# A recurrent retention block with a mixture of experts: TensorE's program written out over the layers instead of looped

## The reference, cut to what matters

```python
xn = _layernorm(x, axis=-1)                  # x: 8 samples x 512 tokens x 128
s = attn(xn)                                 # L = 4 layers, one after the other
g = _silu(ffn(xn))                           # top-1 mixture of 8 experts, 128 -> 512 -> 128
return x + s * g

def block(h, p):                             # one layer of attn, scanned over the 4 layers
    r = _retention(h, wk)                    # k, q, v; tril(q k^T), row sums, times v
    m = r @ w1 + b1
    a, gate = jnp.split(m, 2, axis=-1)
    m = a * jax.nn.silu(gate) @ w2 + b2
    m = _groupnorm1(m, gg, gb)
    y = m + h
    f = jax.nn.gelu(y @ wf1 + bf1_, approximate=False) @ wf2 + bf2_
    return (_layernorm(f + y, lg, lb), None)
```

## Time and profile before

| | us |
|---|---|
| median of 3 runs | 535.2 (534.99 to 535.72) |
| span of the profiled execution, first to last instruction | 533.2 |
| the profiled execution's own time | not recorded apart from its span |
| TensorE matmuls, busy | 478.8 (90% of the span) |
| VectorE, busy | 387.6 (73%) |
| ScalarE, busy | 264.7 (50%) |
| GpSimd, busy | 262.9 (49%) |
| mean granted TensorE clock | 0.958 of full speed |

### The profile page before, as it was taken

One profiled execution on the slowest core, in us unless ns is written; L12 is line 12 of the kernel. 1 busy time (PEld: TensorE's weight loads), 2 busy tenths in 40 slices (PEclk: granted clock), 3 DMA queues, 4 the chain that ended last, 5 costly groups with the idle time before them and its releaser, 6 DMA issues.

```text
span 533.2 us, 11094 instructions
## 1 busy us (share of the span) xinstructions
PE 478.8 (90%) x3179; PEld 399.0 (75%) x3180; DVE 387.6 (73%) x1343; ACT 264.7 (50%) x565; POOL 262.9 (49%) x349
## 2 busy tenths in 40 slices
PE   6998889999999999996999999996999999999610
PEld 4886666667888898884898888884888888986410
DVE  4668888888777777774677777775577777786896
ACT  3823244444555555661556565661466555655630
POOL 4472388886454444441444443442345344434664
PEclk9999999999999999997999999998999999999665
DMA  9999411115111010111011010111011011113213
GB/s 255 235 114 260 131 35 36 36 36 92 51 57 43 34 57 31 56 59 35 22 45 56 31 61 32 55 61 40 6 56 61 32 56 37 55 37 104 65 39 119
DMA packets 48844, 36.30 MB, mean 68 GB/s; under 512 B 13960, under 2 KB 39888, under 8 KB 48784
## 3 DMA queue, kind: packets, MB, share of 16 engines
q1 hardware_dynamic: 45824, 29.73, 22.0%
q0 software_dynamic: 2432, 5.02, 2.9%
q10 hardware_dynamic: 528, 0.79, 0.4%
HBM read 14.85 MB, written 9.84 MB: 46 GB/s over the span
## 4 chain that ended last, share of the span: by engine, by line
PE 70%; POOL 10%; DVE 8%; issue 7%; DMA 2%; ACT 1%; SPq 0%; DVEq 0%; POOLq 0%
PE bank L1358 9%; PE bank L1284 7%; PE bank L1264 7%; POOL x_slots L550 6%; PE pair L1405 4%; PE pair L1387 4%; PE pair L1429 4%; PE bank L1442 4%; PE bank L1295 4%; PE bank L1296 4%; PE bank L1297 4%; PE pair L1383 4%; PE pair L1431 3%; PE bank L1322 3%; PE bank L1356 2%
## 5 line engine op out<-in xcount | busy, mean ns | idle before, releaser
L577 POOL TENSOR_TENSOR zhat<-zhat,lg_l 128x512 f32<-128x512 f32 x31 | 40.7, 1312 | 109.6 <-PE bank L1331 109.5
L1358 PE MATMUL bank<-f_l,G_sb 128*128 128x128 f32 x512 | 74.7, 279 | 0.0
L780 ACT ACTIVATE y_sb<-bank,gn_bi,gn_sc 128x512 f32<-128x512 f32 x32 | 24.9, 778 | 96.3 <-DVE gn_bi L1120 96.3
L1358 PEld LDWEIGHTS bank<-f_l,G_sb 128*128 128x128 f32 x512 | 69.1, 196 | 1.4 <-issue 1.4
L629 POOL DMA_INDIRECT y_rows<-yt,tile_ids x39 | 40.4, 1036 | 58.3 <-DVE yt L1166 44.8
L775 ACT ACTIVATE uT_h<-bank 128x512 fp32r<-128x512 f32 x32 | 19.1, 597 | 98.9 <-PE bank L1341 98.9
L1264 PEld LDWEIGHTS bank<-moe_w,h_T 128*128 128x128 f32 x312 | 39.7, 191 | 15.0 <-issue 15.0
L465 POOL TENSOR_TENSOR ln_rs<-ln_ve,half_neg 128x4 f32<-128x4 f32 x32 | 33.1, 1034 | 30.6 <-DVE ln_ve L804 30.4
L686 ACT ACTIVATE h_T<-bank,w_t 128x128 f32<-128x128 f32 x156 | 44.6, 375 | 4.8 <-PE bank L1284 4.8
L1284 PE MATMUL bank<-xtT,w_t 128*128 128x128 f32 x320 | 44.9, 283 | 0.2
L752 ACT ACTIVATE G_sb<-bank,par 128x512 f32<-128x512 f32 x64 | 42.7, 700 | 3.2 <-PE bank L1322 1.4
(11 more groups left out here) (196 smaller groups left out, 1241.9 us busy)
## 6 DMA issues: line engine op xcount, KB each, us to landing
w_t<-moe_w SPq DMA_DIRECT2D x41, 258.0 KB, 2.3
xt<-x_slots SPq DMA_DIRECT2D x41, 65.0 KB, 1.8
x_slots<-moe_w SPq DMA_DIRECT2D x1, 2644.5 KB, 21.8
x_sb<-in_L_attn_x SPq DMA_DIRECT2D x8, 256.0 KB, 6.0
moe_w<-in_L_ffn_w SPq DMA_DIRECT2D x1, 2048.0 KB, 19.9
moe_w<-y_rows SPq DMA_DIRECT2D x8, 256.0 KB, 5.2
out<-moe_w SPq DMA_DIRECT2D x8, 256.0 KB, 2.2
all_f<-in_L_attn_Wf SPq DMA_DIRECT2D x2, 512.0 KB, 4.5
```

The source lines that it names most:

```text
L1358: last = mm(bank[7][:, at_c], G_sb[:, k, at_c], f2_l[:, k, :], start=False, stop=k == 1)
```

## The change

TensorE alone no longer calls `steps`: Python runs its `step` for each layer with l a number, so that the matmuls of layers 1 to 3 stand in the program three times, one after another. The other engines call what they called before, and every matmul reads the same tiles as before.

```diff
@@ -1460,7 +1460,11 @@
                 if isinstance(l, int) and l == 0 and t == B - 2:
                     pe.wait_ge(route_done, 1)
 
-            steps(pe, step, L, B, LAG)
+            for l in range(L):
+                for t in range(B):
+                    step(l, t)
+            for t in range(LAG):
+                step(L, t)
```

## The result

| | before | after |
|---|---|---|
| median of the runs, us | 535.1 (534.67 to 535.72, 4 runs) | 522.49 (522.34 to 522.77, 4 runs) |
| ratio, 95% interval | | 0.9762 (0.9744 to 0.978) |
| span of the profiled execution, us | 533.2 | 520.4 |
| mean granted TensorE clock | 0.958 | 0.971 |

The changed kernel is 2.4% faster; 523.2 us was forecast. The span fell by 12.8 us, where 12.0 were forecast.

A forecast was written before the change was run, and what follows sets the result against it. TensorE was taken to bound the kernel, stalled at its two jumps back. Span 533.2 us, less 15.6, plus two waits of 1.8 (12.0 off), gives 521.2; the median lies 2.0 above, 523.2 us; range 519.4 to 530.2 us.

The forecast's parts named there:

- The stall and its cause: At TensorE's two jumps back: fetching the loop's head again stalls it 5.05 and 5.28 us, around line 1383.
- The 15.6 us: TensorE's excess at both jumps over the loop's entry, 7.62 + 7.98 us of stalls and slow matmuls, all removed.
- The yardstick: The loop's entry, without a jump back: TensorE takes 2.94 us from line 1383 to line 1405.
- Register instructions at nothing: TensorE's register instructions ahead of most waits, dropped with the loop, cost nothing because its queue covers them.
- The new wait on line 1429: At both jumps TensorE waits 1.8 us for VectorE's mask, late from VectorE's own jump; bounds 0 and 6.2 or 6.5.
- Case E: At both heads VectorE stops for two instruction packets in turn: waits of 3.5 us each, 526.6 us; chance 0.13.
- The sum: Whole kernel: 12.0 us off the span, 533.2 to 521.2 us; the median 2.0 us above, 523.2 us.
- A: At both heads the other engines return in time, VectorE's stall under 1.1 us: 519.6 us; chance 0.18.
- B: TensorE's clock falls behind the wait at line 1429, costing at most 3.4 us each: 530.0 us; chance 0.13.
- C: The gap ahead of line 1383 is the loop head's register work and stays: 535.2 us; chance 0.05.
- ScalarE at nothing: ScalarE's return after its jump, ahead of copying the queries for line 1405, costs 0; bounds 0 and some 6 us.
- D: VectorE's return replaces TensorE's: line 1429 waits up to 6.2 and 6.5 us, clock falls, 539.1 us; chance 0.03.

## Why the prediction was right

**The stall and its cause.** Right, and shown from both sides: the gap goes with the jump and not with the loop's instructions (three loops of one pass, 522.50 us), and a jump to code just behind is free (523.81 us). The packets of q8 follow the gaps: 33, 31, 29 and 27 for two jumps with two gaps each, two with one, one with one, and none.

**The 15.6 us.** Right. The yardstick of 2.94 us from line 1383 to line 1405 was met with 2.93, and the low clock behind the gaps went with them.

**Register instructions at nothing.** Right: with them kept the time is the same to 0.01 us.

**The new wait on line 1429.** Right in place, releaser and sign, and the cost is close: 1.8 us each forecast, 1.68 and 1.62 measured. Two errors of size lie under this and partly cancel. VectorE's return was put too long: I let it take up `S_sb` at 249.0 in the old trace's time, 2.9 us after `zhat`, by TensorE's second stall, and it took 2.46. So the idle time was 1.42 and 1.37 us and not 1.8. And the sum counted a wait as its idle time alone, where some 0.25 us more were lost behind each. The one time that the trace of before could not show was found by the nearest row of the same kind, which served well. Case E, VectorE stopped for its second block as well, did not come: `S_sb` and the mask run in one piece.

**The sum.** The span came out at 520.4 us, 0.8 below the forecast 521.2. Of that 0.3 us are the waits, 0.4 us lie ahead of the loop, where the change does nothing, and 0.1 us is not placed. That the median is within 0.7 us of the forecast is in part luck, since single executions differ by up to 0.4 us in the same layer 0. The chances are added up wrong at one place of the prediction: the forecast with A, B and E has 0.92 and not 0.93, and C has 0.05 and not 0.04.

**ScalarE at nothing.** Right: 0.04 us. Why its jump is free was not tested.

**Rival B, the clock.** It did not come. After 1.42 us of idle time the granted clock stayed at 1.00. To look for a length of idle time above which the clock falls, between 0.91 and 3.14 us, was too simple, though: the last section has an idle time of 3.25 us that left the clock at 1.00, and one of 2.51 us after which it was low.

**Rivals A, C and D.** A would have needed VectorE back in under 1.1 us. C was settled by the one-pass loops. D would have needed it over 5 us late.

## What to carry to other kernels

Where the bounding engine has no idle time inside a long loop's body but a gap labelled "issue" at its head, ask whether its code has to be fetched again at each jump: write that engine alone out, or put up with one gap or two for each jump. Then look at the engine that delivers first after the head, whose own return was hidden until then: here it took 3.3 of the 15.6 us, and writing it out too brought them back. An edit that is worth nothing alone (VectorE's, 535.57 us) can be worth 3.4 us behind another.

## What the runs showed of the hardware that was not expected

A few instructions that do nothing, placed before a loop, changed its time by some 6 us (535.8 to 530.0), because they moved the loop's head; the same 20 left the written-out kernel at 522.4 us. Put directly ahead of the loop, they stopped a busy TensorE for 2.55 us, which is some 0.13 us for each.

The kernels whose TensorE jumps back over a layer vary more from run to run: by 3.5 us for the kernel before (13 runs), 2.3 us with one jump left (4 runs), 2.7 and 7.5 us with the increments (6 and 10 runs). The changed kernel varied by 0.4 us, and none without such a jump by more than 1.3 us (4 or 5 runs each). The mean granted clock of the kernel before went from 0.951 to 0.961 over those 13 runs. Within one execution the clock did not answer to a gap's length alone. Busy time by stretches of the kernel with the 20 increments ahead of the loop, around its three gaps of 2.55, 2.51 and 2.77 us:

```profile
126.00:134.00 8.00, 5.45 (x37) 4.48 (x36) 5.44 (x24) 2.17 (x4) 3.17 (x5) 1.00 0.68 93
245.00:256.00 11.00, 8.49 (x38) 6.00 (x37) 6.05 (x22) 5.96 (x13) 1.81 (x3) 0.84 0.12 39
363.00:376.00 13.00, 10.23 (x63) 7.78 (x62) 8.13 (x30) 6.20 (x13) 4.66 (x7) 1.00 0.10 33
```

The shortest of the three brought the clock down to 0.84 in the mean (full speed is 1.00), the two longer ones did not. In the kernel with the increments at the start it was 0.76 around the gap of 3.85 us and 1.00 around that of 3.25 us:

```profile
242.00:256.00 14.00, 10.15 (x42) 7.31 (x41) 6.46 (x24) 5.86 (x13) 1.91 (x3) 0.76 0.09 31
...
362.00:376.00 14.00, 10.74 (x67) 8.31 (x66) 7.81 (x30) 6.20 (x13) 5.06 (x6) 1.00 0.10 32
```

So part of what a jump costs is whether the clock falls behind it and for how long, and this is not the same each time. What decides it was not tested.
